# Layer 1's relation products on half the array's rows each, in pairs, into four PSUM banks

## The reference, cut to what matters

```python
k = _typed_matmul(h, k_linears, node_type).reshape(n, N_HEADS, D_K)   # 4 heads of 64
q = _typed_matmul(h, q_linears, node_type).reshape(n, N_HEADS, D_K)
v = _typed_matmul(h, v_linears, node_type).reshape(n, N_HEADS, D_K)
q_att = jnp.einsum('nhd,rhde->rnhe', q, relation_att)
v_msg = jnp.einsum('nhd,rhde->rnhe', v, relation_msg)
attn_score = jnp.sum(q_att[etype, col_idx] * k[row_idx], axis=-1)
```

## Time and profile before

| | us |
|---|---|
| median of 3 timed runs | 9224.35 |
| lowest and highest of them | 9222.07, 9230.39 |
| span of the profiled execution | 9684.1 |
| TensorE matmul busy in it | 6558.8 (68%) |
| VectorE busy | 4925.4 (51%) |
| ScalarE busy | 2452.7 (25%) |
| GpSimd busy | 4253.2 (44%) |

### The profile page before, as it was taken

The page is one execution under the profiler, slowest core; times in us unless marked ns, Lnnn a source line. Parts: engine busy times, 40 slices in busy tenths (PEclk is TensorE's granted clock), DMA queues, the critical chain, the costliest instruction groups (busy, mean ns, idle before and its releaser), DMA issues. The chain is left out here.

```text
span 9684.1 us, 146169 instructions
## 1 busy us (share of the span) xinstructions
PE 6558.8 (68%) x32929; PEld 4679.8 (48%) x32930; DVE 4925.4 (51%) x11606; ACT 2452.7 (25%) x6651; POOL 4253.2 (44%) x3778
## 2 busy tenths in 40 slices
PE   2266666646798777776585767776597566666698
PEld 2244444424465555554373555555486344444466
DVE  8633333334322777776516777777412444444433
ACT  0144433322221222222221222222222111111233
POOL 0078777760001666663042555554021466666000
PEclk9988878777898888888697888888699666766799
DMA  2299988880123666664144666665233333334000
GB/s 90 81 186 179 179 174 176 176 178 11 36 119 122 187 187 186 183 187 116 58 118 130 181 176 179 176 180 150 86 104 100 96 103 106 101 102 98 18 10 20
DMA packets 636665, 1221.72 MB, mean 126 GB/s; under 512 B 110509, under 2 KB 408077, under 8 KB 625556
## 3 DMA queue, kind: packets, MB, share of 16 engines
q0 software_dynamic: 311344, 725.84, 31.7%
q1 hardware_dynamic: 318660, 488.22, 16.4%
q10 hardware_dynamic: 6560, 6.55, 0.2%
HBM read 995.43 MB, written 224.77 MB: 126 GB/s over the span
## 5 line engine op out<-in xcount | busy, mean ns | idle before, releaser
L1827 POOL DMA_INDIRECT rows<-l_kv,index_staged x1728 | 1719.7, 995 | 1881.5 <-issue 706.0
L885 POOL DMA_INDIRECT gcn_sums<-out,target x806 | 1308.7, 1624 | 379.6 <-DMA gcn_sums<-out,target 168.4
L1933 PE MATMUL sum<-messages,hot 128*128 128x260 f32 (+1 forms) x3456 | 1136.7, 472 | 202.4 <-issue 89.3
L2671 POOL DMA_INDIRECT rows<-l_h,index_staged x864 | 919.1, 1064 | 529.8 <-issue 460.9
L1933 PEld LDWEIGHTS sum<-messages,hot 128*128 128x128 f32 x3456 | 728.9, 228 | 378.8 <-issue 184.3
L1910 PE MATMUL q<-queries,spread 128*128 x5184 | 773.7, 297 | 141.4 <-issue 75.8
L905 PE MATMUL g<-same,hot 128*128 128x128 f32 x1612 | 320.2, 375 | 611.9 <-DVEq L959 463.3
L2771 PE MATMUL sum<-messages,hot 128*128 128x259 f32 x1728 | 674.3, 547 | 79.7 <-DVE sums L2903 52.7
L1910 PEld LDWEIGHTS q<-queries,spread 128*128 128x128 bf16 x5184 | 527.6, 106 | 359.6 <-issue 220.2
L2061 DVE TENSOR_TENSOR rows<-q,rows 128x512 f32<-128x512 f32 x864 | 569.0, 683 | 174.9 <-DMA rows<-l_kv,index_staged 136.0
L905 PEld LDWEIGHTS g<-same,hot 128*128 128x128 f32 x1612 | 291.2, 278 | 714.0 <-issue 668.8
(11 more groups left out here) (443 smaller groups left out, 11302.3 us busy)
## 6 DMA issues: line engine op xcount, KB each, us to landing
window<-gcn_rows SPq DMA_DIRECT2D x806, 128.0 KB
rel<-slot_rel SPq DMA_DIRECT2D x324, 256.0 KB
l_kv<-stage SPq DMA_DIRECT2D x26, 2048.0 KB, 6.3
src_row<-in_src_row SPq DMA_DIRECT2D x62, 832.0 KB
first_part<-in_L_ffn_first SPq DMA_DIRECT2D x32, 1030.0 KB
rows<-l_kv,index_staged POOLq DMA_INDIRECT x1728
edge_attr<-in_attr SPq DMA_DIRECT2D x124, 208.0 KB
first_part<-in_L_ffn_first SPq DMA_DIRECT2D x32, 514.0 KB
```

Of the source, the lines that this page charges most:

```text
L885: pool.indirect_dma_start(out=copies[m], out_offset=bass.IndirectOffsetOnAxis(ap=target[:, u, j:j + 1], axis=0), in_=out[:, u, j, :], in_o ...
L1827: pool.indirect_dma_start(out=rows[:, u * 2 + n, j, :], out_offset=None, in_=table, in_offset=bass.IndirectOffsetOnAxis(ap=staged[:, u, n ...
L1933: ins = pe.matmul(sum_ps[g % 2][:, 0:W], hot[:, n, j, :], messages[:, n, j, :, :].rearrange("p h d -> p (h d)"), start=r == 0, stop=r == R ...
L2671: pool.indirect_dma_start(out=rows[:, u * 2 + n, j, :], out_offset=None, in_=table, in_offset=bass.IndirectOffsetOnAxis(ap=staged[:, u, n ...
```

## The change

A relation product now has one head: 64 rows, and all 8 relations with 64 columns each, which again are 512 columns. `job(j)` gives tile h, table n, half o and g, the head in the half; g = 0 lies on the array's rows 0 to 63 and goes to ScalarE's copy, g = 1 on rows 64 to 127 and goes to VectorE's. There are still 16 products in a turn and 16 copies of 512 columns. `blocks` is filled as before; only its diagonal blocks are read. The products go round four banks, of which the fourth is that of `m_ps[0]`. Before each even job TensorE waits until both engines have copied all pairs but the last one. The wait for last turn's copies stands ahead of `turn_masked`, and TensorE waits for all of ScalarE's masked copies of the next turn ahead of the first relation product.

```diff
-    R4 = RELS // 2
...
-        r_ps = [ph.ps(f"related{i}", [P, R4, P]) for i in range(3)]
+        spare_ps = ph.ps("related", [P, 3, RELS * HD])
+        r_ps = [spare_ps[:, i, :].rearrange("p (r d) -> p r d", r=RELS) for i in range(3)] + [
+            m_ps[0][:, :, :].rearrange("p y l -> p (y l)").rearrange("p (r d) -> p r d", r=RELS)]
...
-            return j // J, j % 2, j // 2 % 2, slice(j // 4 % 2 * R4, (j // 4 % 2 + 1) * R4)
+            return j // J, j // 2 % 2, j // 4 % 2, j % 2
...
-                        h, _, o, rels = job(j)
+                        h, n, o, g = job(j)
...
-                        act.activation(stage[:, h, rels, 0, o * P:(o + 1) * P], r_ps[j % 3][:, :, :], ACT.Copy
+                        act.activation(stage[:, h, :, n, o * P + g * HD:o * P + (g + 1) * HD], r_ps[j % 4], ACT.Copy
                                        ).then_inc(outs[0], 1)
...
-                        dve.tensor_copy(stage[:, h, rels, 1, o * P:(o + 1) * P], r_ps[j % 3][:, :, :]
+                        dve.tensor_copy(stage[:, h, :, n, o * P + g * HD:o * P + (g + 1) * HD], r_ps[j % 4]
                                         ).then_inc(outs[1], 1)
...
+                    for n in range(2):
+                        pe.wait_ge(outs[n], t * J)
                     if more:
                         turn_masked(t + 1)
                     pe.wait_ge(kv_out, t + 1)
-                    for n in range(2):
-                        pe.wait_ge(outs[n], t * J)
+                    pe.wait_ge(m_out, (t + 2) * M if more else TURNS * M)
                     for j in range(2 * J):
-                        h, n, o, rels = job(j)
-                        if j >= 3:
-                            pe.wait_ge(outs[(j - 3) % 2], t * J + ((j - 3) // 2 + 1))
-                        pe.matmul(r_ps[j % 3][:, :, :], kvT[:, n, o, h * P:(h + 1) * P], blocks[:, n, o, rels, :],
+                        h, n, o, g = job(j)
+                        at = slice(g * HD, (g + 1) * HD)
+                        if j % 2 == 0:
+                            for e in range(2):
+                                pe.wait_ge(outs[e], t * J + max(0, j // 2 - 1))
+                        pe.matmul(r_ps[j % 4], kvT[at, n, o, h * P:(h + 1) * P], blocks[at, n, o, :, at],
                                   start=True, stop=True).then_inc(r_full, 1)
```

## The result

| | us |
|---|---|
| before, median (4 runs) | 9224.17 (9222.07 to 9230.39) |
| after, median (4 runs) | 9173.41 (9160.20 to 9176.28) |
| ratio after to before | 0.9938, 95% interval 0.9924 to 0.9952 |
| forecast | 9161, range 9143 to 9194 |

The account below looks back on a forecast made before the run. TensorE's stream was taken as the bound: twelve full turns saving 5.09 us each (61.1) plus 2.3 in the last turn make 63.4 us, so 9224.35 becomes 9161, range 9143 to 9194.

Parts of the forecast that it names:

- The bound: In typed_tables TensorE's stream, busy throughout a 37.98 us turn, is the bound; what it saves ends the program earlier.
- the tail: After the last turn's last copy: two stores, 6.3 us each one after the other, land at 3092.1 instead of 3094.4.
- Two halves at once: Relation products: a pair on rows 0 to 63 and 64 to 127 streams in 0.86 us, eight pairs in 6.9.
- Entry: Before a turn's first relation product TensorE waits for ScalarE's masked copies: 0.94 us, taken as 1.0; none on the last turn.
- The copy chain: Relation stage: each pair waits for copies of the pair two before; two pairs take 1.90 or 1.91 us, eight 7.45.
- Switch back: From 64-row relation products back to 128 rows at kv: 0.2 us a turn, bounds 0 to 0.4.
- A full turn: Relation products fall from 13.74 to 8.65 us, saving 5.09 a turn; twelve turns save 61.1 us.
- The last turn: DVE's queries delay pair 2; the last copy ends at 3083.3 instead of 3088.1, but stores leave only 2.3 us saved.
- Rival 1: Waits in the relation stage weigh otherwise: 53 to 73 us saved, 9172 to 9151; forecast with this range, chance 0.82.
- Rival 2: Same-half weight loads in the relation stage not hidden: pair 1.24 us, 33 us saved, 9191; chance 0.08.
- Rival 3: The halves' relation products run one after the other: no gain, +14 us, 9239; chance 0.05.
- Rival 4: Gaps and half-height matmuls in each turn lower the granted clock: 4.4 us lost a turn, +57 us, 9281; chance 0.05.

Follow-up runs that it names:

- same_half: The changed kernel with jobs reordered so four products in a row share the same half of the rows; ratio 0.9999 to the kernel before.
- wait_only: The kernel before plus only TensorE's wait for all of ScalarE's masked copies ahead of the first relation product; ratio 1.0020 to the kernel before.
- own_waits: The changed kernel with each relation product waiting only for the copy of its own bank; 9731.86 us, ratio 0.9929 to the kernel before.
- six_banks: The changed kernel with relation products going round six banks and one wait for each product; 9729.81 us, ratio 0.9921 to the kernel before.
- after_again: The changed kernel, unchanged, on another chip; 9728.83 us, ratio 0.9923 to the kernel before.
- before_again: The kernel before, unchanged, run again on another chip; 9805.39 us, ratio 1.0003.
- after_3: The changed kernel, unchanged, on a further chip beside six banks with late waits; 9755.10 us, ratio 0.9933 to the kernel before.
- late_wait: The changed kernel with the wait for masked copies moved to the third relation product and lowered to the third copy; 9733.01 us, ratio 0.9933 to the kernel before.

## Why the prediction was right, and where its terms were off

The bound. TensorE's stream was the bound of the function, and what it saved ended the program earlier. The forecast was 63.4 us. Of the 62.0 us between the functions in the traces of before and after, 1.5 are luck of the clock and 0.9 are given back in the tail (both below), so the change itself is worth 59.6 us by the traces.

Two halves at once. Predicted from the L444 burst and shown by same_half: the pair streams in 0.86 us, and its two products take 0.86 us each when they share a half. Copies of 8 runs of 64 kept their 0.69 and 0.60 us.

Entry. 0.94 from the rows, 1.0 taken; after and wait_only both have 0.85 + 0.10 = 0.95. The other waits queued behind it, for which up to 0.15 was allowed, cost nothing that shows.

The copy chain. This is the term that was too small, by 0.34 us a turn: 7.45 us for eight pairs, where the changed kernel has 7.98 - 0.10 - 0.09 = 7.79. Two pairs take 2.01 us and not 1.91, three times over. The 0.05 us from the end of a copy to the next load belong to a single wait; from the end of DVE's copy to the load after two waits it is 2760.11 - 2759.99 = 0.12, and DVE's copy starts 0.04 later than ACT's. The prediction said that no row isolates what two waits cost, set 0 for the forecast and up to 0.1 for each as the bound (8.05), and the bound held; in own_waits, where the two waits are taken apart, two pairs take the predicted 1.91. Six_banks has 6.88, the lower bound of 6.9, with the chain out of the way.

Switch back. 0.2 predicted; 0.09 ahead of kv and 0.10 in it.

A full turn: predicted 5.09 saved, measured 13.74 - (0.95 + 7.79 + 0.20) = 4.80. By the stages it is 4.79. Twelve of them: 61.1 against 57.5.

The last turn. DVE's queries did hold up pair 2, as predicted. The turn's relation part, to the end of the last copy:

```profile
3019.31:3031.80 12.49, 9.51 (x33) 3.54 (x32) 8.37 (x13) 4.78 (x8) 0.00 (x0) 0.86 0.26 110
```

It was 3088.10 - 3072.57 = 15.53 before (the start 3072.57 is that of the first relation product, the end from the earlier trace rows); 3.0 less, and not 4.8. The granted clock in that stretch is 0.86; the fall is shown in the last section and accounts for 1.45. The tail, from the last copy to the next phase's first load on SP, was predicted 2.5 longer, since two stores now lie closer together. In after that load is issued at 3040.42:

```profile
3040.42 0.81 SPq L1760 DMA_DIRECT2D rel<-slot_rel  x2
```

That is 8.62 after the last copy; before, 3095.82 - 3088.10 = 7.72. The tail grew by 0.9. The prediction had let the two stores land one after the other, 12.6 us from the first issue; here they were issued at 3027.85 and 3031.87, and their traffic ended at 3038.2, after 10.4 us. So 3.0 less 0.9, 2.1 us, remain where 2.3 were forecast: two errors of opposite sign, and their meeting is luck. In after_again, where the clock did not fall, the same stretch is 11.04 us and the tail 8.55, which leaves 3.7. With 57.5 the 2.1 make 59.6 us, and 1.5 more came from a first masked stage in which the granted clock rose from 0.50 earlier (5.92 us in place of 7.42); that has nothing to do with the change.

Rival 1, the forecast's own range of 53 to 73 us, covers the 59.6 of the traces; the 51 of the medians lies 2 us outside it, inside the stated range of the time. Rival 2 (loads exposed) fell in after and in same_half. Rival 3 (no gain) has its number in same_half, where the halves were kept apart: about 0 instead of 51 to 83 us. Rival 4 (the clock) did not happen in the twelve full turns of any version of the changed kernel with pairs; see below for where it did. Its price was added up loosely: 57 us are thirteen times 4.4, while the entry wait and the switch that it contains come in twelve turns only.

Left open: the whole time's own scatter. Nothing here tells 51 from 62 us on the first chip, where no execution of the kernel before near its timed runs was recorded. The prediction allowed for the recorded 9684.1 us being 5% too long within the function too; with turns of 37.98 us in before_again as well, that allowance was not needed. Why the recorded execution was 460 us longer stays open.

## What to carry to other kernels

A block-diagonal product of two 64-row blocks spends half of every product on zeros. Here, in f32, two products of 512 columns on the two halves of the rows, each into its own bank, took the 0.86 us of one. Then the copies out of PSUM are the next chain: count start to result, the longer copy, the waits in a row and the exposed load against the number of pairs in flight, and look for banks that are idle in that stage before accepting a wait. When a bank is borrowed, wait for it ahead of the product that writes it and not ahead of the stage.

## What was not expected of the hardware

In the last turn of after TensorE stood still for 2.24 us, waiting for VectorE, and then worked on at half clock for 3.3 us. The idle time, and the granted clock in the stretches around it:

```profile
3023.54 2.58 PE L2422 MATMUL related<-relation_blocks,kvT 64*128 64x512 f32 x5 [2.24 <-DVE stage L2375]
...
2597.20:3023.80 426.60, 414.22 (x1743) 285.89 (x1744) 119.22 (x175) 108.78 (x174) 0.00 (x0) 1.00 0.28 118
3023.90:3027.20 3.30, 3.30 (x10) 1.54 (x8) 0.90 (x3) 0.79 (x2) 0.00 (x0) 0.50 0.00 0
3027.30:3034.00 6.70, 3.76 (x16) 0.99 (x12) 3.24 (x5) 2.70 (x5) 0.00 (x0) 1.00 0.83 352
```

In after_again, the same kernel on another chip, the same standstill of 2.24 us came before 3015.42, and the clock stayed at 1.00:

```profile
3015.42 1.52 PE L2422 MATMUL related<-relation_blocks,kvT 64*128 64x512 f32 x5 [2.24 <-DVE stage L2375]
...
3011.19:3020.91 9.72, 7.36 (x33) 2.84 (x32) 7.21 (x12) 3.86 (x7) 0.00 (x0) 1.00 0.19 81
```

The same products took 9.72 us there and 11.17 in after: 1.45 us for the fall. In after_3 it fell again, for 3.4 us; in late_wait, with the same 2.24 us before 3004.64, it did not, and the same products took 9.72 us:

```profile
3000.41:3010.13 9.72, 7.36 (x32) 2.85 (x32) 7.21 (x12) 3.85 (x7) 0.00 (x0) 1.00 0.19 81
```

So after the same gap the clock fell in two recorded executions of four. In after, after_again, after_3, own_waits and six_banks, which stand still for 0.69 us once in every full turn, it never fell there.

In same_half, where products of half height follow one another singly, the clock fell once in the middle, though TensorE was busy without a gap in that stretch and in the 2.7 us before it, since the turn's standstill of 0.69 us:

```profile
2927.40:2934.10 6.70, 6.70 (x14) 3.35 (x13) 1.40 (x3) 1.79 (x3) 0.00 (x0) 0.50 0.00 0
```

One such event in one recorded execution; why it fell there stays open. With the halves in pairs no full turn has one, in the eight traces of the five kernels that have pairs.
